# Second attention scores by the path: node tiles 64 columns apart, one register a step, loads of four and three registers a unit early

## The reference, cut to what matters

```python
def _transformer_conv(x, src, dst, edge_attr, wq, bq, wk, bk, wv, bv, we, ws, bs, n_nodes):
    q = x @ wq + bq
    k = x @ wk + bk
    v = x @ wv + bv
    e = edge_attr @ we
    ke = k[src] + e
    score = jnp.sum(q[dst] * ke, axis=-1) / jnp.sqrt(...)
    smax = jax.ops.segment_max(score, dst, num_segments=n_nodes)
    a = jnp.exp(score - smax[dst])
    denom = jax.ops.segment_sum(a, dst, num_segments=n_nodes)
    alpha = a / denom[dst]
    msg = alpha[:, None] * (v[src] + e)
    out = jax.ops.segment_sum(msg, dst, num_segments=n_nodes)
    return out + x @ ws + bs

h1 = jax.nn.relu(_transformer_conv(x, ..., n))
h2 = jax.nn.relu(_transformer_conv(h1, ..., n))
```

## Time and profile before

| | |
|---|---|
| median of 3 runs | 7337.79 us (7335.06 to 7341.6) |
| profiled execution: its time, its span | 7333.15 us, 7330.7 us |
| mean granted clock of TensorE over the span | 0.845 |
| TensorE busy over the span | 4774.7 us (65%) |
| VectorE, ScalarE, GpSimd busy over the span | 4776.5 (65%), 1735.3 (24%), 3433.3 us (47%) |
| L1896 MATMUL: count, busy, idle before | 2,352, 348.6 us, 164.1 us |

### The profile page before, as it was taken

How to read it: one execution, slowest core, us unless ns; L and a number is a source line. 1 busy time by engine, 2 the same in 40 slices (tenths; PEclk the granted TensorE clock), 3 DMA queues, 4 the chain that set the end, 5 groups by cost and what they waited for, 6 DMA issues and landing times. The chain is left out here.

```text
span 7330.7 us, 108466 instructions
## 1 busy us (share of the span) xinstructions
PE 4774.7 (65%) x33331; PEld 4287.2 (58%) x33408; DVE 4776.5 (65%) x6430; ACT 1735.3 (24%) x2361; POOL 3433.3 (47%) x2958
## 2 busy tenths in 40 slices
PE   4665335760388785555555888885668784784797
PEld 2355334650377785555555878875558773674675
DVE  5998544226677786666677855556588783782457
ACT  0043112330134342222222421111134560000001
POOL 0198665770477204777771046620000006766766
PEclk9866668995699997676667999998889997997899
DMA  5198666769522474232333767777747893122009
GB/s 224 31 276 265 153 143 140 143 122 391 216 74 72 129 247 128 79 80 79 79 79 114 249 222 241 241 217 199 198 163 254 318 337 111 51 58 90 14 12 280
DMA packets 1020192, 1194.07 MB, mean 163 GB/s; under 512 B 696673, under 2 KB 758710, under 8 KB 1018622
## 3 DMA queue, kind: packets, MB, share of 16 engines
q1 hardware_dynamic: 694222, 859.74, 37.0%
q10 hardware_dynamic: 193840, 251.55, 10.0%
q0 software_dynamic: 131712, 77.25, 7.3%
HBM read 736.76 MB, written 457.73 MB: 163 GB/s over the span
## 5 line engine op out<-in xcount | busy, mean ns | idle before, releaser
L915 POOL DMA_INDIRECT gc_msgs<-t,src_rows x784 | 754.6, 963 | 1513.0 <-POOLq L150 1219.0
L2316 PE MATMUL gc_ring<-gc_msgs,gc_hot 128*128 x4736 | 649.6, 295 | 242.7 <-SPq L2275 236.8
L2316 PEld LDWEIGHTS gc_ring<-gc_msgs,gc_hot 128*128 128x128 f32 x4736 | 623.2, 209 | 312.7 <-issue 305.0
L969 POOL DMA_INDIRECT acc<-de_sums,de_put x392 | 607.4, 1549 | 313.7 <-issue 151.2
L915 POOL DMA_INDIRECT at1s_ends<-x,src_rows x392 | 395.5, 1009 | 492.0 <-POOLq L150 372.8
L1103 PE MATMUL de_ring<-de_win,de_pick 128*128 x2368 | 342.2, 305 | 264.0 <-DMA de_win<-t 264.0
L1103 PEld LDWEIGHTS de_ring<-de_win,de_pick 128*128 128x128 f32 x2368 | 321.6, 217 | 286.4 <-issue 280.7
L915 POOL DMA_INDIRECT at1s_ends<-x,dst_rows x392 | 419.0, 1069 | 119.5 <-issue 119.5
L915 POOL DMA_INDIRECT re_rows<-x,src_rows x392 | 407.0, 1038 | 125.2 <-issue 124.6
L915 POOL DMA_INDIRECT at2s_ends<-h,src_rows x392 | 378.8, 966 | 180.1 <-issue 112.8
L1896 PE MATMUL at2s_ring<-at2s_win,at2s_hot 128*128 (+1 forms) x2352 | 348.6, 306 | 164.1 <-DVE at2s_hot L1976 74.9
(11 more groups left out here) (499 smaller groups left out, 11742.8 us busy)
## 6 DMA issues: line engine op xcount, KB each, us to landing
rew_win<-x SPq DMA_DIRECT2D x74, 544.0 KB, 4.1
at1w_win<-g SPq DMA_DIRECT2D x74, 544.0 KB, 4.1
at2w_win<-g SPq DMA_DIRECT2D x74, 544.0 KB, 4.2
de_near<-same SPq DMA_DIRECT2D x74, 512.0 KB, 5.1
de_win<-t SPq DMA_DIRECT2D x74, 512.0 KB, 4.4
x<-rew_win SPq DMA_DIRECT2D x74, 512.0 KB, 2.9
h<-at1w_win SPq DMA_DIRECT2D x74, 512.0 KB, 2.8
h<-at2w_win SPq DMA_DIRECT2D x74, 512.0 KB, 2.9
```

What stands on the lines that cost most here:

```text
L915: nc.gpsimd.indirect_dma_start(buf[:, t * width:(t + 1) * width], None, table, bass.IndirectOffsetOnAxis(ap=rows[:, t:t + 1], axis=0)).the ...
L969: nc.gpsimd.indirect_dma_start(g.acc0[j % SUMS], bass.IndirectOffsetOnAxis(ap=put[:, j:j + 1], axis=0), sums[:, j * D:(j + 1) * D], None, ...
L2316: done = nc.tensor.matmul(ring[:, bass.ds(to[n], SLOT)], hot[k][:, n, :], each_group(msgs[:, bass.ds(of[n], MID)], SLOT // MID), start=Fal ...
```

## The change

In `win` the seven node tiles now lie side by side in the first 448 columns, and the 448 columns behind them are zeros. The moving operand of a step becomes two runs of 64 columns, 448 apart: one in the tiles, one in the zeros. Both operands' places are now at 64 r, so one register serves both. `g.rise` holds seven integers a unit in a width of eight. The load is cut in two: four registers (`EARLY`, steps 0 to 3) and three (`LATE`, steps 4 to 6). Each part of the next unit is loaded right behind the matmuls of this unit's same part, where all seven were loaded at the unit's head before. In the loop the parts of `expand` become four and three matmuls instead of three and four. The transfer into `win` has a contiguous destination now, the same bytes as before. Waits and semaphores are the same.

```diff
-        g.rise = keep("rise", [P, 2, 2 * UNIT], i32)
+        g.rise = keep("rise", [P, 2, UNIT + 1], i32)
...
-                    v.tensor_scalar(g.rise[:, h, UNIT:2 * UNIT], rises[:, h * UNIT:(h + 1) * UNIT], 2.0, None, ALU.mult)
...
+    EARLY, LATE = range(4), range(4, UNIT)
...
-                    sp.dma_start(grouped(win[k][:, :], 2 * D)[:, :, 0:D], of[:, bass.ds(tile, UNIT * D)].rearrange("p (t d) -> p t d", d=D)).then_inc(win_in[k], 16)
+                    sp.dma_start(win[k][:, 0:UNIT * D], of[:, bass.ds(tile, UNIT * D)]).then_inc(win_in[k], 16)
...
-                def places(u):
-                    regs = [nc.tensor.alloc_register(f"{name}_rise{u}_{n}") for n in range(2 * UNIT)]
-                    nc.tensor.load(regs, g.rise[u // 2:u // 2 + 1, u % 2, :])
-                    return [pe.snap(x, donate=True, min_val=0, max_val=n % UNIT * D * (1 + n // UNIT)) for n, x in enumerate(regs)]
-
-                def expand(u, at, some):
+                def places(u, some):
+                    if u < UNITS:
+                        regs = [nc.tensor.alloc_register(f"{name}_rise{u}_{n}") for n in some]
+                        nc.tensor.load(regs, g.rise[u // 2:u // 2 + 1, u % 2, some.start:some.stop])
+                        for n, x in zip(some, regs):
+                            at[n] = pe.snap(x, donate=True, min_val=0, max_val=n * D)
+
+                def expand(u, some):
...
-                                                win[k][:, bass.ds(at[UNIT + n], 2 * D)], start=False, stop=(n == UNIT - 1), skip_group_check=True)
+                                                grouped(win[k][:, :], UNIT * D)[:, :, bass.ds(at[n], D)], start=False, stop=(n == UNIT - 1), skip_group_check=True)
                     if UNIT - 1 in some:
                         done.then_inc(expanded, 1)
+                    places(u + 1, some)
...
+                at = [None] * UNIT
+                places(0, EARLY)
+                places(0, LATE)
                 for c in range(TURNS):
                     spread_now = c >= LAG
-                    at = places(c - LAG) if spread_now else None
...
-                        expand(c - LAG, at, range(3))
+                        expand(c - LAG, EARLY)
...
-                        expand(c - LAG, at, range(3, UNIT))
+                        expand(c - LAG, LATE)
...
-                    expand(u, places(u), range(UNIT))
+                    expand(u, EARLY)
+                    expand(u, LATE)
```

## The result

The changed kernel takes 7211.6 us (median of 4 runs, 7206.6 to 7213.7), the kernel before 7337.8 us. The ratio is 0.9827 with a 95% interval of 0.981 to 0.9844, that is 126 us less, with an interval of 114 to 139 us. The profiled execution took 7213.7 us with a span of 7211.8 us, 118.9 us less than the span before.

A forecast was written before the change was run, and what follows sets the result against it. It took the load of 14 registers in TensorE's serial queue to set the tail at 3.48 us a unit. 122 us from the tail and 6 from the loop, 128 off 7337.8, gave 7210 us, range 7198 to 7262.

The forecast's parts named there:

- The price of a load: Register loads on TensorE: EARLY would take 0.33 us and LATE 0.80 us, 1.13 us a unit.
- The loop: Turns where units ride with batches: the load at a turn's head goes, 23 x 0.26 = 6 us; moved loads cost nothing.
- that sign of being wrong: In the loop: the prediction is wrong if own(1) and own(2) start later than 2.08 us after each other.
- The matmul: expand's passes: one register for both operands and a moving operand in two runs of 64 columns cost nothing.
- The tail's pace: The 121 units that run alone: 2.46 us a unit instead of 3.48, so 122 us off.
- The floor of VectorE: In the tail, VectorE's chain of dot, reduce, add and compare allows no less than 2.41 us a unit.
- The remainder for the clock: In the tail, a small rest of slower clock on TensorE's passes, 0.05 us a unit.
- TensorE's queue: In the tail, wait, 14 passes, both loads and gaps take 2.23 us a unit instead of 3.48.
- the landings: Rival: window transfers landing in 6.0 us against three slots set the tail at 2.8 us a unit, 7250 us; chance 0.14.
- The packets: win's transfer in 1,792-byte runs fits at a DMA share of 0.9; if packets brought nothing, 3 to 5 us worse.
- the single fetches: Rival: all seven registers fetched singly, TensorE's queue 2.94 us a unit, 71 us off, 7267 us; chance 0.07.
- the split operand: Rival: two far runs double a pass to 0.22 us, making the kernel 9 us slower, 7347 us; chance 0.04.

The follow-up runs named there:

- layout_only: The kernel before with only the new layout of win, 14 registers still in one load at the unit's head: 7333.1 us, ratio 1.0000.
- seven_wide: The changed kernel with g.rise seven words a unit instead of eight, so that odd units start at byte 28: 7228.1 us in one run.
- late_four: The changed kernel with four words loaded in LATE in place of three: 7212.4 us, ratio 0.9842 to the kernel before.
- old_packets: The changed kernel with win's old 256-byte runs and two registers a step, in two loads of eight: 7231.8 us, ratio 0.9865 to the kernel before.
- four_slots: The changed kernel with a fourth slot for win and kwin, and line's transfer waiting for compare instead of expand: 7178.7 us, ratio 0.9793 to the kernel before.
- head_load: The changed kernel with seven registers in one load at the unit's head, nothing loaded ahead: 7207.8 us, ratio 0.9831 to the kernel before.

## Why the prediction was right, and where it was off

**The cause.** It said that the register load in TensorE's queue set the tail, against the names in the chain of waits. Right: with the loads left long, layout_only gains nothing; with them short, the tail gave 106.5 us.

**The price of a load.** Right, to 0.02 us, and the reading behind it was borne out: fours at a multiple of 16 bytes together, everything else singly (seven_wide, late_four, old_packets with 0.60 us for eight).

**The loop.** 6 us forecast, 5.7 found. The moved loads cost nothing, as costed. The 5.1 us between the loop's last dot and the tail's first were in no term of the sum; layout_only keeps the old interval (10.7), so they come with the loads. In the traces it is the tail's first dot that waited 5.6 us for the ring before and 0.5 after; I did not take it further apart. `own(1)` and `own(2)` start 2.07 us after each other (4879.36 and 4881.43 us), as they did, so that sign of being wrong stayed away.

**The matmul.** Nothing forecast, nothing found.

**The tail's pace.** This is the term that was mis-sized: 2.46 us a unit forecast, 2.59 found, 16 us too much of a gain. Two of its terms were too high. The floor of VectorE was taken as 2.41 us from a stretch that held a hidden wait, and is 2.21. The remainder for the clock was not needed, the clock is at 1.00. One was too low: TensorE's queue, 2.23 forecast, is at most the 2.35 us that four_slots shows. With all three right, the forecast by its own logic would have been about 2.35.

What it put aside came in: the landings, given as a rival with 6 us each and 2.8 us a unit. They stayed at 4.4 us, and still cost 2.57 - 2.35 = 0.22 us a unit, as four_slots shows. This is also where one of its own signs of being wrong came true: VectorE waits in the tail for `kwin`, 57 times, and is busy 80% of it, not 85%.

The formula of that rival allowed 2.27 us at a landing of 4.4 us. It followed `win`, from the end of one expand to the next one in the same slot. The trace has a longer cycle, through the keys. From the end of a unit's passes to the next `line` and behind it to the keys' transfer it is 1.41 us (5105.58 to 5106.99), the keys take 4.2 us to land, from a dot to the end of the compare behind it it is 2.30 us (5104.21 to 5106.51), and the unit of that compare takes 0.10 and 1.89 us to the end of its passes. That unit is the fourth after the first one: 9.9 / 4 = 2.48 us a unit, an estimate from these rows. The cycle through `line`, 0.03 + 4.3 + 0.69 + 0.10 + 1.89 us over three units, comes to 2.34. With a slot more, as in four_slots, the keys' cycle spans five units, 2.0 us a unit, below the other bounds, and the waits for keys did go. The last 0.1 us between 2.48 and 2.57 to 2.59 is not accounted for; keys and lines that land later than their median are the likely cause, not shown.

**The packets.** Forecast at 3 to 5 us through the DMA engines' share, found at 18 us in the tail by old_packets, of which the longer first load has a part. The share was right (0.9 forecast, 0.87 found), and so was the rate that it came from: 266/0.87 = 306 GB/s after, 310 forecast, against 254/0.92 = 276 in old_packets. But the effect goes by the landings, which come on top of a tight slot count.

**The other rivals.** Neither the single fetches (2.94 us a unit) nor the split operand at twice a pass's time came: the loads cost 0.34 and 0.78 us, the passes 275 ns.

**The total.** 128 us forecast against 126: the 16 us too much in the tail are made up in part by the 5 us between loop and tail; the rest is that the medians lie 126 us apart and the two profiled spans 119. That the total agrees so closely is partly luck.

**The skill's rule.** By 200 ns a register ("Runtime: NRT & Kernel Launch", "Instruction fetch mechanics" in the Trainium skill) the tail would have been an estimated 4 us longer than forecast. For loads like these the runs decide against one figure: 84 ns a register in a four that starts at a multiple of 16 bytes (0.335 us), 266 in one that does not (1.064 us).

## What to carry to other kernels

Register loads stand in an engine's own queue and are counted neither as its busy time nor, by name, as its waits; when a stage runs at a pace that no engine's busy time explains, and odd and even turns differ, look at the loads' durations and at the alignment of what they read. A busy time without gaps in one stretch of a timeline is no floor unless the engine's own overlap is seen elsewhere. And when a stall goes, a landing that used to fit in the stall must be set against the number of slots, for every window that a turn needs and in the order in which the issuing queue takes them: here the keys stood behind another window's slot, and a fourth slot was worth 28 us more.

## What the runs showed of the hardware

- A register load costs about 0.07 us and 0.26 us for each four words that start at a multiple of 16 bytes, 0.24 us for each other word: 0.34 us for four, 0.78 for three, 0.60 for eight, 1.08 for seven, 1.06 for four at byte 28. Four words are cheaper than three.
- An instruction of VectorE can start 0.09 us before the one ahead of it is listed as ended.
- A load among a unit's 14 passes stretches them: 1.80 us with none (head_load), 1.89 with one of 0.34 us, 2.17 with one of 0.60 us (old_packets).
- The granted clock of the tail was 0.88 with TensorE idle for up to 2.8 us between units, 0.89 with the new layout and the same loads, and 1.00 when the loads were short.
- The tail's landings moved little with the DMA share. With 1,792-byte runs `win` took 4.1 us at 0.66 (layout_only), 4.4 at 0.87 and 4.4 at 0.93 (four_slots). With 256-byte runs it took 4.4 us at 0.72 (before) and 4.7 at 0.92 (old_packets).
